# A selective-scan block on one core: the gate product goes from VectorE to ScalarE and GpSimd, and the norm statistics from VectorE to ScalarE

## What is computed

```python
xr = x.reshape(B, F, 2, T)                       # rotation by a per-sequence angle
out0, out1 = c*x0 - s*x1, s*x0 + c*x1
xn = (x - mean) * rsqrt(var + 1e-5) * ln_g + ln_b
# for the forward and for the reversed sequence, with the same weights:
xi, z = split(xn @ in_proj)                      # 256 + 256 channels
u = silu(causal_conv4(xi) + conv_b)
dt, Bm, Cm = split(u @ x_proj)                   # 64 + 16 + 16
delta = softplus(dt @ dt_proj + dt_b)
h[n] = exp(delta * A[n]) * h_prev[n] + delta*u*Bm[n]      # n = 0..15
y = sum_n h[n]*Cm[n] + u*D
y = y * silu(z)
# both directions: projection to 128, gelu, gated linear unit, residual
# then: an expert's low-rank feed-forward for each sequence, and a gated
# feed-forward 128 -> 512 -> 512 -> 512 -> 128 with two gelu layers, residual
```

## Time and profile before

| | |
|---|---|
| median of 3 runs | 999.75 us |
| lowest, highest | 999.14, 1003.47 us |
| the profiled execution | 998.47 us |
| its span, first to last instruction | 996.6 us |
| mean granted TensorE clock | 0.974 |
| busy: TensorE, VectorE, GpSimd, ScalarE | 909.4, 894.6, 845.6, 796.5 us |

### The profile page before, as it was taken

How to read it: one execution, slowest core, us unless ns; L and a number is a source line. 1 busy time by engine, 2 the same in 40 slices (tenths; PEclk the granted TensorE clock), 3 DMA queues, 4 the chain that set the end, 5 groups by cost and what they waited for, 6 DMA issues and landing times.

```text
span 996.6 us, 14200 instructions
## 1 busy us (share of the span) xinstructions
PE 909.4 (91%) x4552; PEld 610.2 (61%) x4552; DVE 894.6 (90%) x688; ACT 796.5 (80%) x1294; POOL 845.6 (85%) x427
## 2 busy tenths in 40 slices
PE   5798677879999999999999999999999988999988
PEld 3455546666755676557755666556755775667557
DVE  2899999999999999999999999999999999998610
ACT  6968876988699977998699977898698868888632
POOL 0689999999899998999999898999999999787400
PEclk9799799999999999999999999999999999999999
DMA  4867564754553846556454755557375475565100
GB/s 116 291 205 225 182 193 163 214 185 139 186 167 110 261 145 201 170 174 223 127 181 127 243 164 168 164 183 235 118 246 155 153 196 165 137 206 140 47 1 17
DMA packets 97817, 167.54 MB, mean 168 GB/s; under 512 B 9936, under 2 KB 33552, under 8 KB 97488
## 3 DMA queue, kind: packets, MB, share of 16 engines
q1 hardware_dynamic: 97744, 166.64, 54.5%
HBM read 159.26 MB, written 7.34 MB: 167 GB/s over the span
## 4 chain that ended last, share of the span: by engine, by line
PE 40%; DVE 21%; issue 14%; ACT 14%; POOL 9%; DMA 1%; DVEq 0%; SPq 0%; POOLq 0%; ACTq 0%
DVE bank_d L1025 14%; PE bank_y L1315 9%; PE bank_m L1232 7%; POOL state L637 7%; PE bank_m L1148 6%; PE bank_m L1225 4%; ACT bank_d L796 4%; DVE state L1023 3%; ACT L668 3%; DVE state L1030 2%; PE bank_m L1243 2%; PE bank_m L1174 2%; PE bank_m L1198 2%; POOL state L642 2%; PE bank_m L1207 2%
## 5 line engine op out<-in xcount | busy, mean ns | idle before, releaser
L637 POOL TENSOR_TENSOR state<-du,b_rows 128x1024 f32<-128x1024 f32 (+1 forms) x288 | 622.3, 2189 | 47.3 <-PE bank_y L1315 41.5
L1025 DVE TENSOR_TENSOR_SCAN bank_d<-bank_d,state 128x1024 f32<-128x1024 f32 (+1 forms) x225 | 460.9, 2048 | 10.4 <-ACT bank_d L796 9.4
L796 ACT ACTIVATE bank_d<-delta,a_neg 128x512 f32<-128x512 f32 (+1 forms) x540 | 322.9, 634 | 67.6 <-DVE state L1030 62.2
L1315 PEld LDWEIGHTS bank_y<-ident,state 128*128 128x128 f32 x2048 | 243.6, 145 | 75.1 <-issue 66.0
L1315 PE MATMUL bank_y<-ident,state 128*128 128x128 f32 x2048 | 265.4, 281 | 15.0 <-DVE gated L1041 14.2
L1030 DVE TENSOR_TENSOR state<-bank_d,c_rows 128x1024 f32<-128x1024 f32 (+1 forms) x225 | 248.4, 1104 | 6.7
L642 POOL TENSOR_TENSOR state<-state,c_rows 128x1024 f32<-128x1024 f32 (+1 forms) x63 | 133.8, 2124 | 11.5 <-DVE state L1023 11.4
L1148 PE MATMUL bank_m<-xnT,w_conv 128*128 128x508 f32 (+7 forms) x288 | 117.0, 552 | 2.9 <-DVE x1T L1050 2.2
L1232 PE MATMUL bank_m<-hidA,h_s 128*128 128x512 f32 (+1 forms) x256 | 108.1, 568 | 4.6 <-ACT hidA L868 4.3
L1225 PE MATMUL bank_m<-hidB,h_s 128*128 128x512 f32 (+1 forms) x256 | 107.4, 567 | 0.3 <-DVE hidB L1064 0.2
L1023 DVE TENSOR_TENSOR_SCAN state<-bank_d,state 128x1024 f32<-128x1024 f32 (+1 forms) x45 | 91.9, 2042 | 1.0 <-ACT bank_d L796 1.0
(11 more groups left out here) (148 smaller groups left out, 1040.3 us busy)
## 6 DMA issues: line engine op xcount, KB each, us to landing
b_rows<-bc_store SPq DMA_DIRECT2D x256, 256.0 KB, 5.1
c_rows<-bc_store SPq DMA_DIRECT2D x256, 256.0 KB, 4.8
wsel<-merged SPq DMA_DIRECT2D x32, 512.0 KB, 3.4
merged<-hidA SPq DMA_DIRECT2D x8, 512.0 KB, 3.1
h_s<-in_h SPq DMA_DIRECT2D x2, 1024.0 KB, 8.8
xin<-in_x SPq DMA_DIRECT2D x7, 256.0 KB, 5.4
out<-cT SPq DMA_DIRECT2D x7, 256.0 KB, 3.0
wsel<-in_factors SPq DMA_DIRECT2D x8, 160.0 KB, 3.6
```

What stands on the lines that cost most here:

```text
L637: nc.gpsimd.tensor_tensor(split(unit_state(u)), du[:, d, :, :width(g)], per_half(b_rows, u), ALU.mult).then_inc(S.bx_ready, 1)
L796: ins = act.activation(split(unit_decay(u))[:, h], delta[:, d, h, :width(g)], ACT.Exp, scale=a_neg[:, h, n:n + 1])
L1025: dve.tensor_tensor_scan(decay, decay, drive, 0.0, ALU.mult, ALU.add).then_inc(S.scanned, 1)
L1315: ins = pe.matmul(bank_y[:, h, s * P:(s + 1) * P], split(unit_state(u))[:, h, s * LEN:(s + 1) * LEN], ident[:, :], start=(n == 0 and s == ...
```

## The change

1. In all groups but the last, ScalarE copies the turned y out of PSUM into `gated` (`take_y`, reversed for d = 1, signal y_taken), and GpSimd multiplies it in place by z (`gate_y` on GpSimd). The first sum of the next direction waits for y_taken. The last group keeps the product on VectorE.
2. From group 1 on, the norm statistics come from ScalarE: a copy of each sequence half with an accumulator output (`norm_sums`), then squares about the mean with an accumulator output (`norm_squares`). Group 0 keeps bn_stats and bn_aggr.
3. At the start VectorE also marks the sequence starts of group 0 and makes drive 0; exp(a_log) moves behind the first Ln of the norm; the table for the softplus of group 0 is asked for at the take of dbc0.
4. The places in the tables are other ones throughout, and the timeline starts at -80 in place of -48. `POOL_UNITS`, `AHEAD`, the leads and the groups stay.

```diff
-FILL = {"norm": (-46, -24.5, -33, -26.5, -26, -25.5, -27.5),
+FILL = {"norm": (-71, -27, -32, -26.5, -24.5, -24.5, -26),
...
-        "out": (36.5, 36, 38.5, 37.5, 37, 37.5, 37),
+        "out": (37, 37, 37.5, 37, 38, 38, 39),
...
-          "copied": ((19, 17.5, 18.5, 18.5, 18.5, 17.5, 19), (34, 35, 34, 33, 33, 33.5, 49.5)),
+ACT_AT = {"turned": ((20, 17.5, 20, 20, 20, 18.5, 42.5), (36, 34.5, 33.5, 35, 35, 35.5, 45)),
+          "copied": ((18.5, 17, 19, 18.5, 19, 17.5, 18.5), (34.5, 33, 33, 34, 34, 33, 42.5)),
...
+          "scale": (-65, -73, -42.5, -37.5, -36, -47.5, -47),
+          "softplus": ((-22, -6, -9.5, -6.5, -6.5, -7, -7.5), (5.5, 1.5, 0, 1, 0.5, 0.5, -1.5)),
+          "stats": (-80.5, -64.5, -36.5, -34, -32, -46.5, -38),
+          "aggr": (-80, -57, -34, -31.5, -28, -42.5, -38)}
...
-VEC = {"gated": ((20, 20, 20.5, 21.5, 21.5, 19, 20.5), (35.5, 36, 36, 36, 36, 37, 38)),
+GPS = {"gated": ((20, 18.5, 20.5, 20.5, 20, 34, 15.5), (36, 36, 36.5, 36, 36.5, 36.5, 45)),
...
-FIRST, STEP, END = -48.0, 0.5, 96.0
+FIRST, STEP, END = -80.0, 0.5, 96.0
...
+            def gate_y(g, d):
+                pool.wait_ge(S.y_taken, 2 * g + d + 1)
+                pool.wait_ge(S.z_ready, g + 1)
+                w = width(g)
+                nc.gpsimd.tensor_tensor(gated[:, d, :, :w], gated[:, d, :, :w], z[:, g % 2, :, :w], ALU.mult).then_inc(S.gated_ready, 1)
...
+            def norm_sums(g):
+                act.wait_ge(S.cond_done, g + 1)
+                for t in range(sequences(g)):
+                    ins = act.activation(scaled[:, t // 2, t % 2], xc[:, t // 2, t % 2], ACT.Copy, accum_out=moments[:, t, 0:1])
+                ins.then_inc(S.summed, 1)
+                act.wait_ge(S.summed, g)
+                act.activation(neg_mean[:, :sequences(g)], moments[:, :sequences(g), 0], ACT.Copy, scale=-1.0 / HID).then_inc(S.mean_ready, 1)
+
+            def norm_squares(g):
+                act.wait_ge(S.mean_ready, g)
+                for t in range(sequences(g)):
+                    ins = act.activation(scaled[:, t // 2, t % 2], xc[:, t // 2, t % 2], ACT.Square, bias=neg_mean[:, t:t + 1],
+                                         accum_out=moments[:, t, 1:2])
+                ins.then_inc(S.squares_summed, 1)
...
-                wait(act, S.gated_ready, 2 * g + d)
+                wait(act, S.y_turned, 2 * g + d)
                 act.activation(y_rows[:, :, :width(g)], bank_y[:, :, :width(g)], ACT.Copy).then_inc(S.y_copied, 1)
+
+            def take_y(g, d):
+                act.wait_ge(S.y_turned, 2 * g + d + 1)
+                dst = gated[:, d, :, :width(g)]
+                act.activation(dst[:, :, ::-1] if d == 1 else dst, bank_y[:, :, :width(g)], ACT.Copy).then_inc(S.y_taken, 1)
...
+                if g == 0 and name == "dbc0":
+                    return EXP_LN
...
+                dve.wait_ge(S.du_ready, 1)
+                dve.memset(delta[:, 0, :, :w].rearrange("p h (b t) -> p h b t", t=LEN)[:, :, :, 0:1], FORGET).then_inc(S.starts_marked, 1)
+                wait_row(dve, b_loaded, 0)
+                dve.tensor_tensor(split(unit_state(0)), du[:, 0, :, :w], per_half(b_rows, 0), ALU.mult).then_inc(S.bx_ready, 1)
...
-                        if rel == slot(VEC, g, "gated", d):
+                        if g == NG - 1 and rel == slot(VEC, g, "gated", d):
                             gate_y(g, d)
...
-                if n == 0:
-                    wait(pe, S.gated_ready, 2 * g + d)
+                if n == 0 and g == NG - 1 and d == 1:
+                    pe.wait_ge(S.gated_ready, 2 * g + 1)
+                elif n == 0:
+                    wait(pe, S.y_taken, 2 * g + d)
```

More of the change, by code:

```diff
@@ L142 @@
[L142 to L145 removed]
[5 rows of a table removed]
[L151 to L158 removed]
+FILL = {"norm": (-71, -27, -32, -26.5, -24.5, -24.5, -26),
[12 rows of a table added]
+        "out": (37, 37, 37.5, 37, 38, 38, 39),
+        "glu1": (38.5, 39, 41, 40, 39.5, 38.5, 41),
+        "glu0": (39.5, 39.5, 41.5, 41.5, 41, 39, 41),
+        "res": (39.5, 41, 41.5, 41.5, 41.5, 42.5, 42),
[21 rows of a table added]
+        "tok": (71.5, 73.5, 73.5, 71.5, 70.5, 76.5, 92.5)}
@@ new lines @@
+DECAY_LEAD = 2
+VEC = {"gated": ((39.5, 37, 36, 41, 46.5, 17, 20), (67, 49.5, 48.5, 52.5, 69.5, 58, 43.5)),
[5 rows of a table added]
+GPS = {"gated": ((20, 18.5, 20.5, 20.5, 20, 34, 15.5), (36, 36, 36.5, 36, 36.5, 36.5, 45)),
+       "residual": (-41, -13.5, -19, -14.5, -18, -18, -15.5),
+       "delta": ((-76.5, -4.5, -4.5, -4.5, -5, -4.5, -6.5), (5.5, 3, 6, 9, 2, 7.5, -1)),
+       "inputs": ((-62.5, -4, -4, -3.5, -5, -3.5, -3.5), (11, 6, 6.5, 11.5, 10.5, 7.5, 6)),
+       "mix": (-41.5, -72.5, -40.5, -36, -33, -48, -38)}
@@ L654, in _ @@
                             step_sizes(g, d)
+                        if g < NG - 1 and rel == slot(GPS, g, "gated", d):
+                            gate_y(g, d)
                         if rel == slot(GPS, g, "inputs", d):
@@ L914, in _ @@
             rotation_tables()
-            act.wait_ge(S.a_ready, 1)
             takes = take_plan()
@@ L921, in _ @@
                             copy_y(g, d)
+                        if g < NG - 1 and rel == slot(ACT_AT, g, "turned", d):
+                            take_y(g, d)
                     for layer in range(2):
@@ L929, in _ @@
                         scale_pairs(g)
+                    if g > 0 and rel == slot(ACT_AT, g, "stats"):
+                        norm_sums(g)
+                    if g > 0 and rel == slot(ACT_AT, g, "aggr"):
+                        norm_squares(g)
                     if rel == slot(ACT_AT, g, "power"):
@@ L1003, in first_inputs, with first_moments @@
                 dve.tensor_tensor(du[:, 0, :, :w], delta[:, 0, :, :w], u_f[:, 0, :, :w], ALU.mult).then_inc(S.du_ready, 1)
-            def take_stats(g):
-                dve.wait_ge(S.cond_done, g + 1)
-                for t in range(sequences(g)):
+                dve.wait_ge(S.du_ready, 1)
+                dve.memset(delta[:, 0, :, :w].rearrange("p h (b t) -> p h b t", t=LEN)[:, :, :, 0:1], FORGET).then_inc(S.starts_marked, 1)
+                wait_row(dve, b_loaded, 0)
+                dve.tensor_tensor(split(unit_state(0)), du[:, 0, :, :w], per_half(b_rows, 0), ALU.mult).then_inc(S.bx_ready, 1)
+            def first_moments():
+                dve.wait_ge(S.cond_done, 1)
+                for t in range(sequences(0)):
                     ins = dve.bn_stats(stats[:, t], xc[:, t // 2, t % 2])
                 ins.then_inc(S.stats_done, 1)
-            def aggregate(g):
-                dve.wait_ge(S.stats_done, g + 1)
-                wait(dve, S.xn_ready, g)
-                for t in range(sequences(g)):
+                dve.wait_ge(S.stats_done, 1)
+                for t in range(sequences(0)):
                     ins = dve.bn_aggr(moments[:, t], stats[:, t])
```

102 lines of the change are left out of this document (50 added, 52 removed), and 136 rows, old and new, of tables (FILL, TAKE_LAG, VEC).

## The result

The changed kernel took 1014.8 us (median of 4 runs, 1010.69 to 1017.22), the kernel before 999.44 beside it: ratio 1.0141, 95% interval 1.0115 to 1.0167. It is 1.4% slower; I had said 1002 us, with a range up to 1012. The profiled execution took 1017.22 us, span 1015.4, granted clock 0.971 over it.

The account below looks back on a forecast made before the run. VectorE was taken to set the pace, with GpSimd taking over at the same height after the change. 998.5 + 7.0 (windows) - 0.6 (start) - 1.5 (group 0) - 1.1 (group 8) = 1002.3, said as 1002 us; range 984 to 1012.

Parts of the forecast that it names:

- VectorE sets the pace; its 23 us would be the windows' gain if it alone did.: Seven windows of full-width groups: VectorE, 98% busy, sets the pace; losing 3.3 us per group would save 23 us if alone.
- rival A: GpSimd hides its added product, exclusion staying at 17.5 us: 985.8 us, limit 972 by VectorE's own pace; chance 0.25.
- The pace goes over to GpSimd at the same height, +7.0.: Seven full-width windows: GpSimd becomes the bound, 781.4 us against 774.4, so +7.0 us, bounds -2 and +14.
- The busy part: GpSimd's work in the seven windows: 717.5 without exclusion, plus 31.4 products, plus 28.4 exclusion, less about 5 slipping out: 772.3 us.
- The idle term: GpSimd's idle time in the seven windows: 1.3 us each, as it may run up to eight states ahead; alternative 2.3.
- A full GpSimd pays the exclusion, 28.4 us.: Fourteen scans reading both operands from SBUF: a GpSimd with work queued loses 2.03 us at each, 28.4 against 17.5 before.
- ScalarE costed at nothing, with 17.9 us free per window as cover.: ScalarE's added copies and statistics, 5 us per group, cost nothing; bound 21 us if sums delay a decay once per group.
- Start -0.6: Before the first scan: the first scan starts at 29.8 us in place of 30.43, so -0.6 us, bounds -2 and +1.
- Group 0 -1.5: First half-width group: about 2 us of VectorE time removed, GpSimd gets 1.2; -1.5 us, bounds -4 and +1.
- Group 8 -1.1: Last half-width group's stretch: one full product leaves VectorE, so -1.1 us.
- Tail 0: After the last scan: TensorE's queue of nearly the same matmuls sets it, so no change, bounds -3 and +3.
- Rival B: Full GpSimd delays its product, TensorE stands waiting at `fill_out`: 1009 to 1014 us; chance 0.30, shared with late decays from ScalarE's sums.

Follow-up runs that it names:

- run 7: The changed kernel with GpSimd's product cut to 8 of 512 columns in each half, waits, copies and places kept: 1013.13 us, ratio 1.0102 to the kernel before.

## Why the prediction was wrong

**VectorE sets the pace; its 23 us would be the windows' gain if it alone did.** The reading failed. 98% busy was true, but busy time is what an engine does while others let it, and in the old order with this work cut the time is the same (0.9997, 0.9976 to 1.0018). My sum didn't count the 23 us as gain, but the limit of rival A rested on them, and so did my words that VectorE's relief is real.

**The pace goes over to GpSimd at the same height, +7.0.** This term of the sum failed: the windows took 14.5 us more, twice as much, and GpSimd isn't shown to set their pace. The busy part was 772.3 us by my terms (717.5 + 31.4 + 28.4 - 5) and 763.9 measured. The exclusion on GpSimd stayed at 16.3 us (drives 73 ns over GpSimd's products with C at 2363, 223 times) in place of 28.4, and the products took 29.8, twelve and a half in place of thirteen and a half, since one of group 7 falls behind the boundary: 717.5 + 29.8 + 16.3 = 763.6. The idle term failed: 25.0 us, 3.6 per window, where I took 1.3, the least of the seven windows, by an argument about eight states. With the 2.3 that I named as its other end the sum gives 788.4, and 788.90 was measured; but that is luck: that end was reached by other parts than I had put in it, less exclusion and more idle time. And a GpSimd that gets 30 us back (run 7) gives 2 to 4 us, so its sum isn't what adds up to the window.

**A full GpSimd pays the exclusion, 28.4 us.** Wrong side. The drives' mean fell by 10 ns, the early scans' rose by 944 ns: 13.2 us for VectorE. I had written that the step is wrong if the drives' mean does not rise. A fuller GpSimd is only part of why they rose: 4.8 of the 13.2 us stand with all the moved work cut, and in the old order the early scans took 8.1 us more when VectorE alone was relieved. The rule of the Trainium skill (GPSIMD Engine Reference, Key points), that GpSimd and VectorE contend where VectorE has two SBUF inputs, agrees with these rows. Which of the two would wait I didn't ask.

**ScalarE costed at nothing, with 17.9 us free per window as cover.** The second step that failed. Free time in sum is no cover for a decay that is due in 3.45 us. The bound that I gave, 21 us if the sums come in front of a decay, was near: in the old order the statistics alone cost 28 us. In the new order the statistics cost 5 thousandths once product and copies are cut. About 2 us of that are in the start: the first scan starts at 29.3 to 29.4 us in the three profiled executions without statistics, and at 31.1 to 32.0 in the four with them. The rest isn't the waits for decays; in the windows the early scans are 5.1 us shorter once the statistics go too (45.4 to 40.3). The waits did grow, from 6.0 to 20.9 us in the windows, but they are 20.4 with all the moved work cut; so they come with the new order and a relieved VectorE, and my sum had no term for them. Sizes were right: the copy 1.02 us, sums 0.29 and squares 0.39 apart where I took 0.35, 66 table loads as counted.

**Start -0.6.** Measured +1.6, outside my bounds. My working held up to the drive of unit 0 (forecast scan 29.8; the drive was done at 29.4, the decays began at 29.07), but two merges for the expert's weights, in a table of places that I did not read, now stand ahead of scan 0 and wait for TensorE. **Group 0 -1.5**: measured +2.9, outside my bounds. TensorE is busy 63.06 us there, at a granted clock of 0.83 against 0.88; with all the moved work cut it is 69.3 us at 0.88. **Group 8 -1.1**: +0.4. **Tail 0**: -0.6, right.

**Rival A** is out: GpSimd did not hide its products. **Rival B** was nearest by its number, 1009 to 1014, and its threshold of idle time, 2.3 to 3 us, was passed. Its mechanism, TensorE standing at `out`, is shown only in the old order; in the changed kernel TensorE stands 1.4 us there, so its number came out near by luck.

**What stays open.** Which engine or wait holds the changed kernel's windows: that the moved work is the cost is shown, a single hold is not. Why both orders stop at 1000 us without the work. Not VectorE (0.9997), and ScalarE's silus and gelus are 5 to 6 us of it. GpSimd waits about 24 us in the old order's windows for TensorE's sums, and TensorE is busy 719 of 777 us by modelled ends; that the ring of states between the two holds them is argued, not shown, and no run cut TensorE's work. Nor is it shown which places of the new order made the loss in group 0.

## What to carry to other kernels

In a schedule written by hand, take the work away before you move it: the kernel before with the product and statistics cut would have said in one run that there was nothing to win, whatever the engine's 98%. Price an instruction by what is due behind it in its queue, not by the engine's free time in sum: statistics of some 3 us per group cost 28 us in the old order. Cut suspects in pairs too, since product and copies together showed 7 us where neither alone showed a saving clear of the noise. And look in the trace of such a cut for the wait that it was meant to remove: here the waits for decays were all still there.

## What the runs showed of the hardware

**The exclusion can fall on either engine, and for several instructions on end.** A scan with both operands in SBUF lasted 7.61 us in place of 2.28 beside three queued GpSimd instructions, while the drive behind such a scan took 4.36 in place of 2.33 before.

**An accumulator output is an instruction of its own.** Each sum has an ACTIVATION_READ_ACCUMULATOR of 0.19 us behind it, though starts lie only 0.29 us apart for sums and 0.39 for squares, so it is mostly overlapped.

**Time and granted clock go together in part from run to run in the new order.** With ScalarE's parts cut, the profiled run of 1003.16 us had a granted clock of 0.981 over its span, those of 1017.67 and 1018.51 had 0.965 and 0.966; but one of 1008.84 had 0.969 and one of 1016.7 had 0.970. The group 0 of the profiled run took 67.93 us at 0.93 with TensorE busy 56.76 us:

```profile
29.35:97.28 67.93, 56.76 (x255) 34.75 (x253) 61.77 (x70) 55.66 (x119) 58.40 (x47) 0.93 0.75 238
```

The changed kernel took 71.76 us there at 0.83. The clock is granted at 1.2 or 2.4 GHz, so 0.93 is 14% of the stretch at the lower level and 0.83 is 34%. The kernel before varied by 5 to 9 us from run to run, the changed one with ScalarE's parts cut by 15. Which is cause and which is effect, the runs don't tell.
